# Norm scale of the gated MLP moved behind the gate and up products, its weight multiplied into the gate and up weights on ScalarE

## The reference, cut to what matters

```python
def rmsnorm(x, w):
    return x * jax.lax.rsqrt(jnp.mean(x * x, axis=-1, keepdims=True) + EPS) * w
...
for l in range(L):
    h = rmsnorm(x, norm1_w[l])
    x = x + delta_attn(h, Wq[l], Wk[l], Wv[l], Wb[l], Wo[l], onorm_w[l])
    h = rmsnorm(x, norm2_w[l])
    gy = h @ Wg[l]
    g, y = jnp.split(gy, 2, axis=-1)
    x = x + jax.nn.silu(g) * y @ Wd[l]
```

## Time and profile before

| | |
|---|---|
| median of 3 runs | 403.05 us (402.88 to 404.66) |
| the profiled execution | 402.49 us |
| its span in the trace | 400.7 us |
| granted TensorE clock, mean share of full | 0.872 |
| TensorE busy | 310.2 us, 77% of the span |
| VectorE busy | 201.9 us, 50% |
| ScalarE busy | 87.7 us, 22% |
| GpSimd busy | 44.1 us, 11% |

### The profile page before, as it was taken

The page is one execution under the profiler, slowest core; times in us unless marked ns, Lnnn a source line. Parts: engine busy times, 40 slices in busy tenths (PEclk is TensorE's granted clock), DMA queues, the critical chain, the costliest instruction groups (busy, mean ns, idle before and its releaser), DMA issues.

```text
span 400.7 us, 9465 instructions
## 1 busy us (share of the span) xinstructions
PE 310.2 (77%) x4346; PEld 228.6 (57%) x4346; DVE 201.9 (50%) x349; ACT 87.7 (22%) x181; POOL 44.1 (11%) x33
## 2 busy tenths in 40 slices
PE   0999459968972597794776999895676999878965
PEld 0556355757862385472775767573676757555442
DVE  3029977994677443107553222107653232169992
ACT  1132012202210023452111133344121122231120
POOL 0744940200403000000000000000000000000000
PEclk9999958999995578899596799998695699989998
DMA  8999900000000000000000030410000000000001
GB/s 186 334 324 212 362 10 1 2 0 1 2 0 0 0 0 2 0 0 2 3 0 3 2 106 2 151 71 2 3 0 3 2 0 2 1 1 0 2 0 33
DMA packets 2521, 18.26 MB, mean 46 GB/s; under 512 B 441, under 2 KB 761, under 8 KB 1729
## 3 DMA queue, kind: packets, MB, share of 16 engines
q1 hardware_dynamic: 2497, 17.91, 14.6%
HBM read 17.58 MB, written 0.33 MB: 45 GB/s over the span
## 4 chain that ended last, share of the span: by engine, by line
PE 47%; DVE 31%; DMA 9%; ACT 5%; POOL 4%; issue 3%; SPq 1%; DVEq 0%; ACTq 0%; POOLq 0%
PE ps L1221 9%; DMA big<-in_patches 9%; PE ps L1066 5%; PE ps L1217 5%; PE ps L1006 4%; PE ps L1364 3%; POOL xs L262 3%; PE ps L1285 2%; PE ps L1327 2%; DVE big L888 2%; PE ps L1304 2%; PE ps L1016 2%; DVE big L916 2%; DVE qa L569 2%; DVE wt L913 2%
## 5 line engine op out<-in xcount | busy, mean ns | idle before, releaser
L1016 PE MATMUL ps<-big,cwb 120*128 120x384 f32 x120 | 43.6, 523 | 10.3 <-DMA big<-in_patches 10.3
L1016 PEld LDWEIGHTS ps<-big,cwb 120*128 120x128 f32 x120 | 24.4, 207 | 27.1 <-issue 14.3
L1217 PE MATMUL ps<-cst,ones 128*128 128x320 f32 x112 | 37.7, 488 | 0.0
L1066 PE MATMUL ps<-wkvg,pecT 128*128 128x256 f32 x144 | 32.0, 381 | 4.8 <-ACT big L360 4.8
L1221 PE MATMUL ps<-cwb,wl 128*128 128x320 f32 x120 | 33.2, 434 | 0.0
L1066 PEld LDWEIGHTS ps<-wkvg,pecT 128*128 128x128 f32 x144 | 27.0, 190 | 8.6 <-DVE prod L684 3.7
L1217 PEld LDWEIGHTS ps<-cst,ones 128*128 128x128 f32 x112 | 24.0, 219 | 10.6 <-issue 3.9
L1221 PEld LDWEIGHTS ps<-cwb,wl 128*128 128x128 f32 x120 | 22.6, 190 | 10.4 <-issue 0.9
L1285 PE MATMUL ps<-wt,big 32*32 32x32 f32 x1280 | 16.2, 209 | 13.2 <-DVE wt L891 10.5
L262 POOL TENSOR_TENSOR xs<-xs,big 120x640 f32<-120x640 f32 x14 | 23.0, 1645 | 8.2 <-DMA big<-in_patches 7.3
L1285 PEld LDWEIGHTS ps<-wt,big 32*32 32x32 f32 x1280 | 14.5, 121 | 15.3 <-DVE wt L891 11.4
(11 more groups left out here) (224 smaller groups left out, 483.8 us busy)
## 6 DMA issues: line engine op xcount, KB each, us to landing
big<-in_patches SPq DMA_DIRECT2D x6, 900.0 KB, 26.0
wl<-in_layers SPq DMA_DIRECT2D x2, 2176.0 KB, 27.0
wt<-in_tok SPq DMA_DIRECT2D x1, 2304.0 KB, 17.6
wf<-in_ffn SPq DMA_DIRECT2D x1, 2112.0 KB, 26.3
wl<-in_layers SPq DMA_DIRECT2D x2, 1040.0 KB, 23.2
cwb<-in_conv SPq DMA_DIRECT2D x1, 600.0 KB, 5.1
out<-h SPq DMA_DIRECT2D x5, 64.0 KB, 2.0
cst<-in_constants SPq DMA_DIRECT2D x1, 304.0 KB, 39.6
```

The costliest lines, as they stand in the source:

```text
L1016: last = mm(ps[:, i % 4, 0:GRP], cwc[:, k, c * P:(c + 1) * P], xg[:, g, k, :], start=(k == 0), stop=(k == KC - 1))
L1066: last = mm(ps[:, 2 * w + un % 2, t * C:(t + 1) * C], pecT[:, c, i * P:(i + 1) * P], wkvg[:, c, w * C:(w + 1) * C], start=(c == 0), stop=( ...
L1217: mm(ps[:, bank, 0:NT], ones[:, :], cst[:, 0:NT], start=True, stop=True)
```

## The change

The gate and up products take the unscaled xT. Norm weight w goes into wg: on ScalarE, after the l2 norms' last Exp and ahead of the first level copy, two ACTIVATE Copy instructions of 128x1408 with a scale for each partition, in place in wg, behind a wait for wg's load. The scale rs of a token is multiplied on VectorE onto the gate product (into sg) and onto the up product (into act) as they leave PSUM; Silu then works on sg in place, and a third multiply on VectorE makes act = act * sg, one unit behind. The norm's sum on TensorE moves behind the first unit and into bank 6; the four idle-filling matmuls ahead of the projections and the two VectorE instructions of `normed` for this norm go.

```diff
@@ -196,7 +196,7 @@
         EACH = {
-            "lwa": 16, "lwb": 16, "x": 4, "n_sq": 2, "n_ms": 2, "n_rs": 4, "h": 4, "k_mm": 1, "q2_mm": 1, "bt_mm": 1,
+            "lwa": 16, "lwb": 16, "x": 4, "n_sq": 2, "n_ms": 2, "n_rs": 4, "h": 2, "wgs": 2, "gs": FC, "ys": FC, "k_mm": 1, "q2_mm": 1, "bt_mm": 1,
             "v_mm": 1, "silu": 10, "ss_mm": 2, "rkq": 4, "kq": 5, "wbx": 1, "ap_mm": 3, "ap": 3, "y_mm": 2 * (LEVELS - 1), "pairs": 8, "y": 2 * (LEVELS - 1),
@@ -420,7 +420,7 @@
                 act_.wait_ge(S["n_ms"], EACH["n_ms"] * l + half + 1)
-                rsqrt(act_, rs[:, :], ps[:, 0, 0:NT], "n_rs", EPS_RMS, k=2 * half + 1, layer=l)
+                rsqrt(act_, rs[:, :], ps[:, 6 * half, 0:NT], "n_rs", EPS_RMS, k=2 * half + 1, layer=l)
@@ -451,6 +451,11 @@
+                act_.wait_ge(S["lwb"], EACH["lwb"] * l + 16)
+                for c in range(CH):
+                    nc.scalar.activation(wg[:, c, :], wg[:, c, :], ACT.Copy,
+                                         scale=vec[:, V_N2 + 2 * l + c:V_N2 + 2 * l + c + 1]).then_inc(S["wgs"], 1)
                 for lev in range(1, LEVELS):
@@ -470,13 +475,11 @@
                 for i in range(FC):
-                    act_.wait_ge(S["up_mm"], EACH["up_mm"] * l + i + 1)
-                    if i >= 2:
-                        act_.wait_ge(S["act"], EACH["act"] * l + i - 1)
+                    act_.wait_ge(S["gs"], EACH["gs"] * l + i + 1)
                     if i < FC - 1:
-                        nc.scalar.activation(sg[:, i % 2, :], ps[:, i % 3, 0:NT], ACT.Silu).then_inc(S["sg"], 1)
+                        nc.scalar.activation(sg[:, i % 2, :], sg[:, i % 2, :], ACT.Silu).then_inc(S["sg"], 1)
                     else:
-                        nc.scalar.activation(sg[64:P, i % 2, :], ps[0:64, i % 3, 0:NT], ACT.Silu).then_inc(S["sg"], 1)
+                        nc.scalar.activation(sg[64:P, i % 2, :], sg[0:64, i % 2, :], ACT.Silu).then_inc(S["sg"], 1)
@@ -855,16 +858,16 @@
-            def normed(l, half, at):
-                dve.wait_ge(S["n_rs"], EACH["n_rs"] * l + 2 * half + 2)
-                dve.wait_ge(S["x"], EACH["x"] * l + 2 + 2 * half)
+            def normed(l, at):
+                dve.wait_ge(S["n_rs"], EACH["n_rs"] * l + 2)
+                dve.wait_ge(S["x"], EACH["x"] * l + 2)
                 for c in range(CH):
...
             def layer(l):
-                normed(l, 0, V_N1)
+                normed(l, V_N1)
@@ -944,12 +947,26 @@
                     v.tensor_tensor(xT[:, j, :], xT[:, j, :], ps[:, 3 + j, 0:NT], ALU.add).then_inc(S["x"], 1)
-                normed(l, 1, V_N2)
-                for i in range(FC):
+                def gated(i):
+                    dve.wait_ge(S["ys"], EACH["ys"] * l + i + 1)
                     dve.wait_ge(S["sg"], EACH["sg"] * l + i + 1)
                     r = slice(0, P) if i < FC - 1 else slice(64, P)
+                    v.tensor_tensor(act[r, i, :], act[r, i, :], sg[r, i % 2, :], ALU.mult).then_inc(S["act"], 1)
+                dve.wait_ge(S["n_rs"], EACH["n_rs"] * l + 4)
+                for i in range(FC):
+                    dve.wait_ge(S["up_mm"], EACH["up_mm"] * l + i + 1)
+                    if i >= 2:
+                        dve.wait_ge(S["act"], EACH["act"] * l + i - 1)
+                    r = slice(0, P) if i < FC - 1 else slice(0, 64)
+                    v.tensor_tensor(sg[r, i % 2, :], ps[r, i % 3, 0:NT], rs[r, :], ALU.mult).then_inc(S["gs"], 1)
+                    r = slice(0, P) if i < FC - 1 else slice(64, P)
                     b = 3 + i % 3 if i < FC - 1 else i % 3
-                    v.tensor_tensor(act[r, i, :], sg[r, i % 2, :], ps[r, b, 0:NT], ALU.mult).then_inc(S["act"], 1)
+                    v.tensor_tensor(act[r, i, :], ps[r, b, 0:NT], rs[r, :], ALU.mult).then_inc(S["ys"], 1)
+                    if i:
+                        gated(i - 1)
+                gated(FC - 1)
                 for j in range(CH):
@@ -1209,16 +1226,16 @@
                 pe.wait_ge(S["n_sq"], EACH["n_sq"] * l + half + 1)
-                norm_sum(ps[:, 0, 0:NT], sqx[:, :, :], ones[:, :]).then_inc(S["n_ms"], 1)
+                norm_sum(ps[:, 6 * half, 0:NT], sqx[:, :, :], ones[:, :]).then_inc(S["n_ms"], 1)
...
-            def project_to(bank, w, j):
-                for c in range(CH):
-                    last = mm(ps[:, bank, 0:NT], w(c, j), hT[:, c, :], start=(c == 0), stop=(c == CH - 1))
+            def project_to(bank, w, j, x=hT):
+                for c in range(CH):
+                    last = mm(ps[:, bank, 0:NT], w(c, j), x[:, c, :], start=(c == 0), stop=(c == CH - 1))
                 return last
@@ -1341,21 +1358,22 @@
                 keep_clock(5, 2)
-                norm(l, 1)
-                keep_clock(5, 4)
                 pe.wait_ge(S["lwb"], 16 * l + 16)
-                pe.wait_ge(S["h"], EACH["h"] * l + 4)
-                pe.wait_ge(S["n_rs"], EACH["n_rs"] * l + 3)
+                pe.wait_ge(S["wgs"], EACH["wgs"] * l + 2)
+                pe.wait_ge(S["x"], EACH["x"] * l + 4)
                 for i in range(FC):
                     if i >= 3:
-                        pe.wait_ge(S["act"], EACH["act"] * l + i - 2)
+                        pe.wait_ge(S["ys"], EACH["ys"] * l + i - 2)
                     if i < FC - 1:
-                        project_to(i % 3, lambda c, j: wg[:, c, i * P:(i + 1) * P], 0)
-                        last = project_to(3 + i % 3, lambda c, j: wg[:, c, 640 + i * P:640 + (i + 1) * P], 0)
+                        project_to(i % 3, lambda c, j: wg[:, c, i * P:(i + 1) * P], 0, xT)
+                        last = project_to(3 + i % 3, lambda c, j: wg[:, c, 640 + i * P:640 + (i + 1) * P], 0, xT)
                     else:
-                        last = project_to(i % 3, lambda c, j: wg[:, c, 1280:1408], 0)
+                        last = project_to(i % 3, lambda c, j: wg[:, c, 1280:1408], 0, xT)
                     last.then_inc(S["up_mm"], 1)
+                    if i == 0:
+                        norm(l, 1)
                 pe.wait_ge(S["on"], EACH["on"] * l + 1)
+                pe.wait_ge(S["n_rs"], EACH["n_rs"] * l + 3)
                 pe.wait_ge(S["zeros"], 2)
```

## The result

The changed kernel takes 398.97 us, the median of 4 runs (398.60 to 399.35), against 403.86 for the kernel before (4 runs, 402.88 to 405.31): a ratio of 0.988, with an interval of 0.985 to 0.992. The profiled execution took 399.23 us, with a span of 397.1. Two later comparisons gave 0.992 (0.989 to 0.995) and 0.990 (0.988 to 0.992). All executions together: before 402.95 (median of 35, 401.99 to 405.31), changed 399.06 (median of 17, 398.10 to 401.73), 3.9 us or 1% less. Medians here leave out executions more than 1.5% above the fastest of their kernel, which are three of the 12 of `b_fill4` (405.68, 405.71 and 408.14) and two of the six of `l_early_fill3` (400.24 and 400.61), and none of the others.

The account below looks back on a forecast made before the run. TensorE and VectorE were taken to bound the kernel in turn, with the norm's 4.3 us of small steps before the MLP. 402.49 less 5.5 (2.75 a layer) gave 397.0, from the median 397.55; 397.3 was taken, range 395.4 to 400.0.

Parts of the forecast that it names:

- the rival of the clock: Low clock stretches fall differently once layer 1 and the tail move: plus or minus 1.6 us; a loss gives 398.9, 10%.
- TensorE's gain: MLP: first product 3.90 us earlier, less 1.08 for the norm's records, so 2.82; 2.75 a layer after the stall.
- VectorE's tail: End of the MLP: seven products after the fifth unit, step 0.517 or 0.40, stalling the down products 0.12 to nothing; 0.07 taken.
- VectorE becomes the bound: MLP: all 18 VectorE products at step 0.74, stall 2.15 us, gain only 0.7 a layer: 401.1 us; 5%.
- ScalarE's Copies: Ahead of the level copies: two of 1.38 us, 2.8 together, hidden in 8.47 us of each layer, costing nothing.
- The slower rival: Ahead of layer 1's level copies, ScalarE waits for wg's load: 399.5 or 418.8 us by landing time; 2%.
- The start of the sum: Whole kernel: the profiled 402.49 us, with the median shown 0.56 higher; 397.3 lies between the resulting 397.0 and 397.55.
- The sign that it named: Profile after: layer 1 longer than before in stages the change doesn't touch would show the clock made the forecast wrong.

Follow-up runs that it names:

- b_fill4: The changed kernel with the four idle-filling matmuls put back ahead of the MLP's first unit: 403.83 us (median of 9 of its 12 executions).
- l_early_fill3: The changed kernel with the first unit begun on the first addition to xT, and three idle-filling matmuls for five behind the layer's solution: 395.91 us, ratio to before 0.981.
- h_copies4: The changed kernel with eight Copies of 128x1408 on ScalarE in place of two: 398.86 us in its one execution.
- g_scalefirst: The changed kernel with wg's load wait and the two Copies at the head of the layer's ScalarE work, ahead of the projections' Silu: 402.34 us, one execution.

## Why the prediction was right, and where it was off

The direction, the mechanism and the range held: 397.3 was forecast, 395.4 to 400.0 the range, 398.97 the result. The number itself came out on the rival of the clock (398.9, 10%) and not on the forecast (80%).

- **TensorE's gain** held. The first product comes right behind the filling, as worked out. 2.75 us a layer was predicted and 2.85 measured.
- **VectorE's tail**: a stall of 0.07 was taken; the down products took 6.68 in place of 6.62, so 0.06. In the first units products stepped by 0.40 to 0.41 (239.24 to 239.65), the lower end; in the tail, where it counts, by 0.52 (248.27, 248.79, 249.31), the value that was taken. Both kinds of product took 0.48 to 0.49, so the shorter figures of the Trainium skill, "VectorE: DVE Perf Modes", section on the TRN2 errata, are not what this trace shows. Nor did any product run at the dearer rate of the rival *VectorE becomes the bound*. The tail was as close as the sum said: two short gaps of 0.30 and 0.22 in the weight loads.
- **ScalarE's Copies**: 1.4 us each and nothing on the path, as predicted. What was wrong is the room they have: it was read as ScalarE's idle time of 8.47 us, and `h_copies4` showed it to be at least 1.7 us longer.
- **The slower rival** (ScalarE waits for layer 1's load) did not come up. Provoked in another place, in `g_scalefirst`, a wait of 4.07 us went with a loss of 0.4. The prediction priced it in the levels, at every microsecond from 277.5 on; a late load was not tried there, but by `h_copies4` the first 1.7 us would be free.
- **The clock** is the term that was mis-sized. The sum put it at zero, with 10% for a loss of 1.6 us as a rival. The first result was 1.7 us above the forecast, and over all executions 3.9 of the 5.7 us arrived, a loss of 1.8. Of these, 0.3 lie outside the span, which the prediction didn't consider. The rest goes, as far as the traces show, with low stretches of the clock: a tail of 52.71 in all three traces of the changed kernel against 50.7 in two of three before, and a front that ranges from 163.0 to 167.3. The start of the sum is not to blame: 402.49 and 403.05 lie within half a microsecond of the median of all 35 executions, as that trace's short front came with a long tail. The prediction let low stretches fall differently only behind layer 0's MLP; they also did in the front, ahead of everything that the change touches. The sign that it named, layer 1 longer in stages that the change doesn't touch, came with 0.26 us in the first pair of traces (68.90 for 68.64). The Trainium skill, "TensorE: Matmul & The Clock Gate", Part 1, has the windows of the gate free-running; that one kernel, unaltered, draws fronts of 163.0, 164.5 and 167.1 agrees. That the range held is thus partly luck: its 1.6 us for the clock came from one pair of rows, while the front alone spans 4.1 us in the kernel before.

## What to carry to other kernels

A factor that is one number for each token can be multiplied behind a product as well as ahead of it, and the steps that make it then run beside the product: worth the length of that chain less what of it stays in TensorE's row (here 3.9 us less 1.08 for the norm's sum), if the engine that now does the scaling has room in the shadow of TensorE. When a wait goes, look at what had been put into it as filling, since it is on the path from then on, and look whether the first product can start on the first half of its operand. Compare the stage that was changed, cut at fixed instructions in the trace, rather than the total: here the stage told 0.01 us and the total about 1. Then look at the total all the same: a third of what the stage gained did not arrive there.

## What the runs showed that was not expected

- The 16 records of one product took 3.69, 5.38 or about 6.5 us in executions of code that was the same there, for granted clocks of 1.00, 0.91 and 0.81 over 84 to 102 us. The totals of one kernel spread by over 3 us.
- Copies on ScalarE that outlasted its idle time by 1.7 us cost nothing: eight of 128x1408 (2.81 us for the first two, 7.69 for the other six) in place of two.
- ScalarE can be held for 4.07 us by a load while TensorE works through its projections, with a loss of 0.4 us in the one trace of it.
- The time outside the span was 1.7 to 1.9 us in every execution of the kernel before and 2.1 to 2.2 in every one with the change.
- TensorE stood still for 1.42 us inside one product of the levels in one trace of 14, with nothing in the profile that it waited for.
